# Half of the shift's reads issued from GpSimd's queue instead of ScalarE's, in an attention and MLP kernel

## The reference

```
xn   = layernorm(x)
z    = layernorm(xn) * ln_g + ln_b
q, k, v = z @ Wq + bq, z @ Wk + bk, z @ Wv + bv        # 16 heads of 8 columns
p    = sinusoidal_pe(512, 128) @ Wp
content = (q + u_bias) . k           # 512 x 512 for each sequence and head
pos     = relative_shift((q + v_bias) . p)
attn    = softmax((content + pos) * 8**-0.5)
out     = x + (attn . v) @ Wo + bo + ffn(xn)           # ffn: three layers of +-1 weights, relu
relative_shift: pad each 512 x 512 score matrix by one zero column to 512 x 513,
                view it flat as 513 x 512, and drop the first row
```

## Time and profile before

| | |
|---|---|
| runs, median | 1458.58 us |
| profiled execution, its own time | 1458.94 us |
| its span, first to last instruction | 1457.1 us |
| TensorE busy | 1444.8 us (99%) |
| VectorE busy | 1332.3 us (91%) |
| ScalarE busy | 1226.5 us (84%) |
| GpSimd busy | 726.7 us (50%) |
| DMA | 550.41 MB, mean 378 GB/s |
| granted TensorE clock, mean | 0.996 of full speed |

### The profile page before, as it was taken

The page is one execution under the profiler, slowest core; times in us unless marked ns, Lnnn a source line. Parts: engine busy times, 40 slices in busy tenths (PEclk is TensorE's granted clock), DMA queues, the critical chain, the costliest instruction groups (busy, mean ns, idle before and its releaser), DMA issues.

```text
span 1457.1 us, 41448 instructions
## 1 busy us (share of the span) xinstructions
PE 1444.8 (99%) x16113; PEld 962.1 (66%) x16113; DVE 1332.3 (91%) x3489; ACT 1226.5 (84%) x1365; POOL 726.7 (50%) x721
## 2 busy tenths in 40 slices
PE   8999999999999999999999999999999999999999
PEld 5566666666666666666666666666766666666666
DVE  6799999999999999999998999999999998989996
ACT  5688888888888888888888888888888888888874
POOL 5455465554655556455554555456455554533410
PEclk9899999999999999999999999999999999999999
DMA  5999999999999999999999999999999999999992
GB/s 175 390 393 397 379 394 394 389 396 374 403 383 392 400 377 400 381 394 394 383 400 382 400 386 384 401 376 395 388 394 386 385 398 388 396 377 387 393 404 105
DMA packets 80868, 550.41 MB, mean 378 GB/s; under 512 B 9377, under 2 KB 10529, under 8 KB 15137
## 3 DMA queue, kind: packets, MB, share of 16 engines
q1 hardware_dynamic: 43376, 278.61, 49.2%
q10 hardware_dynamic: 37296, 269.15, 48.1%
HBM read 274.57 MB, written 273.15 MB: 376 GB/s over the span
## 4 chain that ended last, share of the span: by engine, by line
PE 97%; ACT 1%; DMA 1%; DVE 1%; issue 0%; ACTq 0%
PE ps_pt L831 36%; PE ps_av L845 19%; PE ps_pos L807 15%; PE ps_job L734 12%; PE ps_job L691 4%; PE ps_job L698 4%; PE ps_job L713 2%; PE ps_job L721 1%; PE ps_job L709 1%; PE ps_job L704 1%; ACT pt_sb L500 1%; DMA shift<-pos_sb 1%; PE ps_av L683 1%; PE ps_con L819 1%; PE ps_job L715 0%; PE ps_job L717 0%
## 5 line engine op out<-in xcount | busy, mean ns | idle before, releaser
L658 DVE CUSTOM_DVE_ANT_0 sc_sb<-ps_con,sc_sb 128x512 f32<-128x512 f32 x1024 | 662.5, 683 | 92.6 <-PE ps_con L819 89.5
L486 ACT COPY pos_sb<-ps_pos 128x1024 f32<-128x1024 f32 x510 | 518.4, 1016 | 189.9 <-PE ps_pos L807 186.6
L666 DVE TENSOR_SCALAR sc_sb<-sc_sb,nmax 128x512 f32<-128x512 f32 x1024 | 601.9, 620 | 0.1
L831 PE MATMUL ps_pt<-c_sb,sc_sb 128*128 128x128 f32 x4048 | 553.5, 280 | 1.9 <-ACT pt_sb L500 1.1
L500 ACT ACTIVATE pt_sb<-ps_pt 128x1024 f32<-128x1024 f32 x506 | 519.4, 1027 | 12.6 <-PE ps_pt L831 12.5
L831 PEld LDWEIGHTS ps_pt<-c_sb,sc_sb 128*128 128x128 f32 x4048 | 433.9, 141 | 126.6 <-issue 94.0
L845 PE MATMUL ps_av<-pt_sb,v_sb 128*9 128x128 f32 x8192 | 319.9, 274 | 0.1
L845 PEld LDWEIGHTS ps_av<-pt_sb,v_sb 128*9 128x9 f32 x8192 | 172.8, 90 | 207.8 <-issue 205.6
L389 POOL CAST h<-act_sb 128x512 fp32r<-128x512 f32 x128 | 82.4, 644 | 392.6 <-ACT act_sb L462 392.3
L807 PE MATMUL ps_pos<-p_stack,q_stack 26*128 26x512 f32 x1024 | 259.3, 497 | 3.3 <-ACT pos_sb L486 3.0
L819 PE MATMUL ps_con<-k_stack,q_stack 26*128 26x512 f32 x1024 | 259.8, 497 | 0.0
(11 more groups left out here) (110 smaller groups left out, 984.4 us busy)
## 6 DMA issues: line engine op xcount, KB each, us to landing
shift<-pos_sb SPq DMA_DIRECT2D x256, 1026.0 KB, 9.1
sc_sb<-shift ACTq DMA_DIRECT2D x256, 1024.0 KB, 9.6
x_sb<-in_x SPq DMA_DIRECT2D x16, 256.0 KB, 11.9
out<-x_sb SPq DMA_DIRECT2D x15, 256.0 KB, 10.8
c_sb<-in_consts ACTq DMA_DIRECT2D x1, 288.0 KB, 6.5
o_t<-in_wp SPq DMA_DIRECT2D x1, 256.0 KB, 5.7
stack_w_sb<-in_stack_w ACTq DMA_DIRECT2D x1, 256.0 KB, 5.4
heads<-in_pe_t SPq DMA_DIRECT2D x1, 256.0 KB, 6.6
```

What stands on the lines that cost most here:

```text
L486: act.copy(to, ps_pos[:, :, :]).then_inc(s_pe, 1)
L658: dve.tensor_tensor_reduce(sc_sb[:, m % N_SC, t, :], ps_con[:, k, :], sc_sb[:, m % N_SC, t, :], -SCALE, 3.4e38, ALU.add, ALU.min, nmax[:, ...
L666: dve.tensor_scalar(sc_sb[:, m % N_SC, t, :], sc_sb[:, m % N_SC, t, :], nmax[:, m % N_SC, t:t + 1], None, ALU.subtract).then_inc(s_sub, 1)
L831: last = pe.transpose(pt_banks(k)[:, j % 2, t * P:(t + 1) * P], sc_sb[:, u % N_SC, t, j * P:(j + 1) * P], id_sb)
```

## The change

The read is put into a function, and it is issued for even units by ScalarE, in half 2u+8 as before, and for odd units by GpSimd, in half 2u+7 of GpSimd's own program, ahead of that half's splits. The two waits and the transfer are the same.

```diff
+        def read(eng, u):
+
+            eng.wait_ge(s_out_w[u % N_POS], 16 * (u // N_POS + 1))
+            wait(eng, s_pt, 2 * (u - N_SC + 1))
+            eng.dma_start(sc_sb[:, u % N_SC].rearrange("p t c -> p (t c)"), chunks(shift[u % N_SHIFT, S:S + S * S])) \
+               .then_inc(s_in[u % N_SC], 16)
...
             for h in HALVES:
+                u, i = half_of(h, SHIFT_H - 1)
+                if i == 0 and u % 2:
+                    read(pool, u)
                 for name, b, c in taken(h):
                     if (name, b, c) in ACTS:
                         split(name, b, c)
...
             for h in HALVES:
                 u, i = half_of(h, SHIFT_H)
-                if i == 0:
-                    act.wait_ge(s_out_w[u % N_POS], 16 * (u // N_POS + 1))
-                    wait(act, s_pt, 2 * (u - N_SC + 1))
-                    act.dma_start(sc_sb[:, u % N_SC].rearrange("p t c -> p (t c)"),
-                                  chunks(shift[u % N_SHIFT, S:S + S * S])) \
-                       .then_inc(s_in[u % N_SC], 16)
+                if i == 0 and u % 2 == 0:
+                    read(act, u)
```

## The result

| | before | changed |
|---|---|---|
| median of the runs timed together | 1458.29 us (1456.28 to 1461.08, 4 runs) | 1473.37 us (1468.08 to 1478.25, 4 runs) |
| ratio, 95% interval | | 1.0093 (1.0071 to 1.0116) |
| profiled execution, own time / span | 1458.94 / 1457.1 us | 1475.6 / 1473.8 us |

The profiled execution of the changed kernel is 2.2 us above its median, so its span shows 16.7 us more than before where the medians show 15.1. The ratio, taken over the runs, would give 13.6 us, with an interval of 10.4 to 16.9.

A forecast was written before the change was run, and what follows sets the result against it. It took TensorE, busy 99% of the span and 97% of the chain, to bound the kernel. Own time 1458.94, -1.0, +0, +0, +4.7 = 1462.6 us, stated as 1463, range 1456 to 1486.

The forecast's parts named there:

- descriptor work holding VectorE: On VectorE's subtraction: GpSimd's work to issue a read makes the subtraction stand still, +4.7 us.
- rival B: In the DMA queues: transfers get in each other's way, writes land late and TensorE loses 18 us, 1477; chance 0.12.
- part 4's worst bound: At VectorE's subtractions: issues of 1.28 us with a margin of 0.13 us, 76 hits, +39 us.
- Part 1: On ScalarE: 128 issues leave it, mostly hidden under a move; gain taken as 1.0 us.
- Part 2: On GpSimd: 128 issues of 1.04 us each, 133 us more on a half-busy engine, hidden; cost 0.
- Part 3: Start of odd reads: 2.2 us earlier mid-kernel, worth 0; in the head at most 0.7 lost, 0.5 gained; taken as 0.
- Part 4: GpSimd against VectorE's subtraction: reads' descriptor work holds it in 67 hits of 0.07 us, +4.7 us; chance 0.44.
- Rival A: On GpSimd and VectorE: descriptor work does not hold VectorE or fits the margins, all hidden, 1458.5 us; chance 0.34.

The follow-up runs named there:

- e1_wait_only: Kernel before, all reads still on ScalarE; GpSimd only waits where the changed kernel has its odd reads and issues nothing: 1460.38 us, 0.9998.
- e6_sync_even: Changed kernel with even reads issued by SyncE behind the write of the unit three steps on, odd ones still on GpSimd: 1479.58 us, 1.0128 against before.
- e5_all_early: Changed kernel with all 256 reads issued by GpSimd at the change's early place, none by ScalarE: 1469.9 us, 1.0057 against the kernel before.
- e8_hw_late: No read on GpSimd; ScalarE issues odd reads later than in the kernel before, behind the exponential of half 2u+8: 1459.74 us, 0.9999 against before.
- e4_sync: Changed kernel with odd reads issued by SyncE behind the write of unit u+2, instead of by GpSimd: 1461.6 us, 1.0012 against the kernel before.
- e11_after_less: Changed kernel with ScalarE's even reads a quarter shorter from unit 12 on: 1461.82 us, 1.0013 against the kernel before.
- e12_before_less: Kernel before with the same even reads a quarter shorter, all reads on ScalarE: 1457.7 us, 0.9984 against the kernel before.
- e7_sixth: Changed kernel with only one read in six (43) issued by GpSimd, the other 213 by ScalarE: 1467.23 us, 1.0046 against the kernel before.
- e10_hw_early: Changed kernel with odd reads issued by ScalarE in half 2u+7, GpSimd keeping only its two waits: 1467.94 us, 1.0051 against the kernel before.
- e2_late: Changed kernel with GpSimd issuing the odd reads one half later, in half 2u+8: 1519.6 us, 1.0407 against the kernel before.
- e3_all_gpsimd: Changed kernel with all 256 reads issued by GpSimd, one half later, none by ScalarE: 1535.8 us, 1.0518 against the kernel before.
- e9_sync_early: Changed kernel with odd reads issued by SyncE right ahead of the write of unit u+2, GpSimd keeping its two waits: 1658.8 us, 1.135 against before.

## Why the prediction was right, and where it was not

The direction (slower, 0.50) and the range (1456 to 1486) held; the time came out 10 us above 1463, and the loss is more than three times the 4.4 us forecast. The mechanism forecast, descriptor work holding VectorE, was the wrong one. That the direction was right all the same is luck, and the range reached so far only because rival B and part 4's worst bound were in it.

- **Part 1** (ScalarE gains 1.0 us): its rows halved, and the transposes' wait for the exponential stayed at 10.2 us. The gain was 0, well inside the bounds.
- **Part 2** (an issue of 1.04 us): 0.60 us, near the lower bound. "Before the next split GpSimd idled 2.93 us, cost 0" looked only at the issue, and at a unit whose write lands at 712.6, long before the next split's source. It left out that the wait inside the read moves the issue: where the write lands about when the source is there, GpSimd's idle time is used up before the issue begins, and the split is late by the issue and by what the wait has run over (0.60 + 0.23 us at 224 us). This zero is the step that failed first.
- **Part 3** (2.2 us earlier, worth 0): in the middle that holds for units whose write has landed, but 83 of 128 reads waited, and in the median, by TensorE's work, an odd read is issued only 0.8 us earlier than before. In the head the later start was not worth 0.7 us at most: VectorE waited 4.27 us for unit 3's read, and 1.3 us of the loss is there.
- **Part 4** (descriptor work holds VectorE, +4.7 us): line 672 was to sum to 649 us and sums to 619.1. And it sums to 621.1 in e1_wait_only, where GpSimd issues nothing. Where an issue alone overlaps a subtraction, it takes 495 ns for 476: 19 ns, 2 us for all 108 of them. So those 17 us come from splits that moved, and the issues' share is small. The collisions that count are real, but they are splits against pairs, as at 224.89, not issues against pairs.
- **Rival B** came nearest to the mechanism, at a chance of 0.12. It said that transfers get in each other's way, that it decides at a landing median of about 10.5 us, and that ScalarE then waits. The median is 10.5 and ScalarE waits (8.7 us in 9 waits). Its price of 18 us stands against 15.1 measured, but the nearness is no proof of its sum: the median does not go with the loss (9.4 us in e6_sync_even, which loses most of the versions with the early reads, 9.8 in e1_wait_only, which loses nothing). Two more of its steps were off. A third queue is not needed (e5_all_early, e6_sync_even); that GpSimd's packets take longer, which B had only as an aside, is seen in two runs (3.12 and 3.09 us a MB) and hardly in the changed kernel (2.70). And "a late write also delays GpSimd's read, so the overlap closes itself" was an argument against B that should have been one for it, since the splits stand behind that read.
- **Rival A** rested on transfers that are alike whoever issues them, and they are not. The Trainium skill ("DMA: Bandwidth & Descriptors", Issuing engines are not separate DMA queues) has it that another issuer saves issue time alone. For SyncE in place of ScalarE the runs agree (1.0012); for GpSimd they don't (in the same half, 1.0407 where ScalarE as issuer has 0.9999).

What is shown: the loss depends on GpSimd being the issuer, not only on when the read is issued. In the later half the ratio is 1.0407 with GpSimd and 0.9999 with ScalarE; in the change's own half it is 1.0093 with GpSimd and 1.0051 with ScalarE, so there about half of the loss goes with the issuer and the other half stays. And most of it goes with room in the transfer engines (15.1 us become 4.1). No single count in the table goes up with the loss:

| run | reads by GpSimd | ratio | landing of writes, median us | splits over 0.4 us late | GpSimd's wait for writes, us | ScalarE's |
|---|---|---|---|---|---|---|
| before | 0 | | 9.1 | 5 | 0 | 3.2 |
| e1_wait_only | 0 | 0.9998 | 9.8 | 15 | 32 | 6.4 |
| e8_hw_late | 0 | 0.9999 | 9.6 | 3 | 0 | 4.0 |
| e4_sync | 0 | 1.0012 | 8.4 | 2 | 0 | 5.2 |
| e11_after_less (against e12_before_less) | 128 | 1.0028 | 9.2 | 17 | 118 | 3.1 |
| e7_sixth | 43 | 1.0046 | 10.1 | 7 | 59 | 3.9 |
| e10_hw_early | 0 | 1.0051 | 9.2 | 5 | 2 | 6.5 |
| e5_all_early | 256 | 1.0057 | 9.9 | 84 | 175 | 1.1 |
| changed | 128 | 1.0093 | 10.5 | 44 | 203 | 8.7 |
| e6_sync_even | 128 | 1.0128 | 9.4 | 73 | 229 | 12.1 |
| e2_late | 128 | 1.0407 | 10.4 | 59 | 28 | 6.2 |
| e3_all_gpsimd | 256 | 1.0518 | 10.3 | 71 | 19 | 0.7 |
| e9_sync_early | 0 | 1.135 | 12.4 | 100 | 539 | 259.9 |

GpSimd's wait is counted in full only where it issues the read itself. e2_late and e3_all_gpsimd lose by late reads (VectorE waits 51 and 123 us for them), e9_sync_early by its own wait on SyncE.

What is only argued: how the loss divides between late splits, GpSimd's issue time ahead of them and ScalarE's own waits; why 256 early reads on GpSimd lose no more than 128; and what costs 7 us in e10_hw_early, where hardly a split is late. ScalarE's waits speak for a share of their own (1.1 us with 256 such reads, 12.1 in e6_sync_even), e1_wait_only's 6.4 at no loss against it. No version with the full reads beat the kernel before; the best (e1_wait_only, e8_hw_late) are level with it.

## What to carry to other kernels

Before a transfer moves to another engine's queue, look at what the wait in front of it will hold up: an idle engine is free to issue, but not free to stand still if other engines time their work by it. In this kernel, where the queues' shares add up to 98% of the span, a change of issuer changed landing times too, so forecast those and not issue times alone. A wait row can be misread: much of the 203 us took the place of other waits of the same engine, and only the start of the work behind it, against the moment its source was ready, tells. And an average row (line 672's sum) can rise by 19 us at no cost, or by 17 with a loss of 15: only where the extra time falls tells.

## What the runs showed of the hardware

- A DMA of 1024 KB issued by GpSimd takes 0.53 to 0.78 us of its time, 0.60 as median, where one on ScalarE's sequencer takes 0.52.
- By the shares of the queues, reads issued by GpSimd take the 16 engines 3.1 us a MB where ScalarE's in the same execution take 2.5 (e2_late, e11_after_less). In the changed kernel the two read 24.6% x 1473.8 / 134.23 = 2.70 and 2.63. The median packet of 8 KB takes 309 ns for both; the difference is in a tail of long packets.
- A subtraction of VectorE's from SBUF to SBUF takes 476 ns on average with GpSimd idle, 495 (at most 610) beside GpSimd's issue of a read, and 804 (up to 1586) beside its splits and norms.
